# Weighted output rows summed as 512-column identity products, with the top's part added on VectorE

## What is computed

```python
logits = x @ W_in.T + b_in                      # 4 trees, 1365 nodes each, 4 outputs ("fan") a node
act4 = gelu(logits).reshape(B, 4, 1365, 4)
decisions = argmax(act4, axis=-1)               # the child to go to
# walk down 5 levels: 6 visited nodes per tree and row
masked = act4 * visited[..., None]
g = masked.reshape(B, -1) @ W_out.T             # sum of gelu(logit) * output row, over visited nodes
x = x + s * silu(g)
```

## Time and profile before

| | us |
|---|---|
| median of three executions | 2034.4 |
| the profiled execution | 2048.09 |
| its span, first to last instruction | 2046.3 |
| mean granted TensorE clock | 0.890 |
| busy in the span: PE / DVE / POOL / ACT | 1549.5 / 1517.5 / 1301.7 / 1129.3 |

### The profile page before, as it was taken

The page is one execution under the profiler, slowest core; times in us unless marked ns, Lnnn a source line. Parts: engine busy times, 40 slices in busy tenths (PEclk is TensorE's granted clock), DMA queues, the critical chain, the costliest instruction groups (busy, mean ns, idle before and its releaser), DMA issues. The chain is left out here.

```text
span 2046.3 us, 31347 instructions
## 1 busy us (share of the span) xinstructions
PE 1549.5 (76%) x10312; PEld 1086.4 (53%) x10376; DVE 1517.5 (74%) x2701; ACT 1129.3 (55%) x3167; POOL 1301.7 (64%) x1780
## 2 busy tenths in 40 slices
PE   6989898888998748731578777777778777777765
PEld 4667677677776643311355555555555555555543
DVE  2466759677686863995688888888888888888843
ACT  2356566665666733331356666666666666666643
POOL 0455446365555710554888888888888888888700
PEclk9889889998999878965689999999999999999877
DMA  2555565564756814763000000000000000000004
GB/s 84 180 179 205 172 216 193 180 207 166 244 170 207 281 50 128 234 178 112 1 15 3 17 17 17 17 6 12 17 17 17 16 6 12 17 17 17 4 3 123
DMA packets 137573, 191.97 MB, mean 94 GB/s; under 512 B 65730, under 2 KB 94788, under 8 KB 137284
## 3 DMA queue, kind: packets, MB, share of 16 engines
q0 software_dynamic: 36864, 134.76, 19.5%
q1 hardware_dynamic: 95314, 50.98, 9.1%
q10 hardware_dynamic: 5234, 4.23, 0.7%
HBM read 166.22 MB, written 23.72 MB: 93 GB/s over the span
## 5 line engine op out<-in xcount | busy, mean ns | idle before, releaser
L304 POOL DMA_INDIRECT l_rows<-in_table,l_idx x256 | 333.9, 1304 | 294.5 <-DVE l_idx L635 179.4
L437 PE MATMUL l_acc<-l_rows,ident 128*128 128x128 f32 x2048 | 310.4, 307 | 73.9 <-ACT l_rows L531 67.5
L437 PEld LDWEIGHTS l_acc<-l_rows,ident 128*128 128x128 f32 x2048 | 275.8, 214 | 109.1 <-ACT l_rows L531 100.7
L531 ACT ACTIVATE l_rows<-l_rows,l_act 128x128 f32<-128x128 f32 x1024 | 306.1, 387 | 2.1
L1315 ACT ACTIVATE lo_prob<-lo_s_ps,lo_nmx,lo_rn 128x128 f32<-128x128 f32 x512 | 226.7, 460 | 43.5 <-DVE lo_nmx L1579 41.7
L1467 POOL TENSOR_TENSOR lo_c<-lo_c 128x1024 f32<-128x1024 f32 x64 | 150.8, 2356 | 11.2 <-DVE lo_c L1569 6.8
L585 DVE TENSOR_TENSOR l_rows<-l_rows,xn_tok 128x2048 f32<-128x2048 f32 x64 | 145.9, 2279 | 8.5 <-DMA l_rows<-in_table,l_idx 8.5
L586 DVE TENSOR_REDUCE l_dot<-l_rows 128x16 f32<-128x2048 f32 x64 | 146.3, 2286 | 2.2
L403 PE MATMUL l_S<-top_out,l_AT 128*128 128x144 f32 (+3 forms) x832 | 126.4, 301 | 21.6 <-ACT l_AT L522 17.2
L522 ACT ACTIVATE l_AT<-l_log,top_bias 128x512 f32<-128x512 f32 (+1 forms) x96 | 63.9, 684 | 133.4 <-PE l_log L395 118.6
L403 PEld LDWEIGHTS l_S<-top_out,l_AT 128*128 128x128 f32 (+2 forms) x832 | 112.2, 202 | 34.5 <-ACT l_AT L522 22.6
(11 more groups left out here) (266 smaller groups left out, 3972.4 us busy)
## 6 DMA issues: line engine op xcount, KB each, us to landing
scratch_ops<-pr_ops SPq DMA_DIRECT2D x4, 1568.0 KB, 5.7
lo_de_ops<-scratch_ops SPq DMA_DIRECT2D x16, 392.0 KB, 3.7
l_rows<-in_table,l_idx POOLq DMA_INDIRECT x256
lo_de_qo<-scratch_qo SPq DMA_DIRECT2D x16, 256.0 KB, 3.9
x_tok<-in_x SPq DMA_DIRECT2D x8, 256.0 KB, 5.2
scratch_q<-pr_stage_q SPq DMA_DIRECT2D x8, 256.0 KB, 3.8
scratch_k<-pr_stage_k SPq DMA_DIRECT2D x8, 256.0 KB, 2.3
pr_Yq<-scratch_q SPq DMA_DIRECT2D x8, 256.0 KB, 3.0
```

The source lines that it names most:

```text
L304: pool.indirect_dma_start(rows[L][:, r % SLOTS, p, :], None, a[f"table{L}"], bass.IndirectOffsetOnAxis(ap=at[:, p:p + 1], axis=0)).then_in ...
L437: ins = pe.matmul(out, m["ident"][:], rows[L][:, r % SLOTS, p, (FAN + f) * D:(FAN + f + 1) * D], start=False, stop=(L == 5 and k == PICK - ...
L531: ins = act.activation(z, z, ACT.Copy, scale=actv[L][:, r % 2, k:k + 1])
```

## The change

1. A product now spans 512 columns: for each of the 4 trees one product of the identity with the 4 scaled output rows of that tree (4 x 128 columns next to each other). Per tile and level there are 4 products instead of 16. `acc[k]` becomes a bank per tile (alternating by r mod 2), and holds four partial sums of 128 columns each; levels 4 and 5 of a tile add into the same bank.
2. The product of the identity with `ftop` is gone. A new DVE step `total(r)` reduces the four partial sums (128x512 from PSUM, read with a step of 128) to 128 columns in SBUF, and adds them to `ftop` of that tile, in place. It runs in round r+2, after `dots(5, r+1)` and ahead of `scan` and `norms`.
3. `ftop` has 3 group buffers instead of 2. `tanh_f` waits for `total` and reads `ftop` (SBUF); so does the merge.
4. Since levels 4 and 5 of one tile share a bank that only alternates by tile, PE's `spread_rows(4, .)` moves one round later: round r now does `spread_rows(4, r-1)`, in the same place of the round, and `spread_rows(5, r-1)` at its end. It waits for `total(r-3)`.
5. To make room, `t1` and `t2` become halves of `fsum`, and `th` shares the buffer of `n_`.

The gathers' own code is unchanged: `gather(4, r+2)` still waits for `spread_rows(4, r-1)`, with 3 buffers.

```diff
-        acc = [ps(f"l0_acc{k}", [P, GT, D]) for k in (0, 1)]
+        acc = [ps(f"l0_acc{k}", [P, FAN * D]) for k in (0, 1)]
@@ TensorE
             def spread_rows(L, r):
-                h, j = r // GT, r % GT
-                out = acc[h % 2][:, j, :]
-                if L == 4:
-                    if j == 0 and h >= 2:
-                        pe.wait_ge(acc_read.sem, acc_read.after(h - 2))
-                    pe.wait_ge(ftop_kept.sem, ftop_kept.after(h))
-                    pe.matmul(out, m["ident"][:], ftop[:, h % 2, j, :], start=(j == 0), stop=False, skip_group_check=True)
-                for k in range(PICK):
-                    if k % 4 == 0:
-                        pe.wait_ge(scaled[L].sem, scaled[L].after(r, k // 4 + 1))
-                    p, f = k // FAN, k % FAN
-                    ins = pe.matmul(out, m["ident"][:], rows[L][:, r % SLOTS, p, (FAN + f) * D:(FAN + f + 1) * D],
-                                    start=False, stop=(L == 5 and k == PICK - 1), skip_group_check=True)
+                if L == 4 and r >= 2:
+                    pe.wait_ge(acc_read.sem, acc_read.after(r - 2))
+                for p in range(TREES):
+                    pe.wait_ge(scaled[L].sem, scaled[L].after(r, p + 1))
+                    ins = pe.matmul(acc[r % 2][:], m["ident"][:], rows[L][:, r % SLOTS, p, FAN * D:2 * FAN * D],
+                                    start=(L == 4 and p == 0), stop=(L == 5 and p == TREES - 1), skip_group_check=True)
                 ins.then_inc(spread[L].sem, 1)
@@
-                if tile_ok(r):
-                    spread_rows(4, r)
+                if tile_ok(r - 1):
+                    spread_rows(4, r - 1)
@@ ScalarE
             def keep_ftop(h):
-                if h >= 2:
-                    act.wait_ge(spread[4].sem, spread[4].after((h - 1) * GT - 1))
+                if h >= 3:
+                    act.wait_ge(merged.sem, merged.after(h - 3))
@@
             def tanh_f(h):
-                act.wait_ge(spread[5].sem, spread[5].after(h * GT + GT - 1))
+                act.wait_ge(totalled.sem, totalled.after(h * GT + GT - 1))
-                act.activation(t_[:], acc[h % 2][:], ACT.Tanh, scale=0.5).then_inc(t_ready.sem, 1)
+                act.activation(t_[:], ftop[:, h % 3], ACT.Tanh, scale=0.5).then_inc(t_ready.sem, 1)
@@ VectorE
+            def total(r):
+                h, j = r // GT, r % GT
+                dve.wait_ge(spread[5].sem, spread[5].after(r))
+                dve.tensor_reduce(fsum[:, 0:D], acc[r % 2][:].rearrange("p (f d) -> p d f", d=D), AX.X, ALU.add).then_inc(acc_read.sem, 1)
+                dve.wait_ge(acc_read.sem, acc_read.after(r))
+                dve.wait_ge(ftop_kept.sem, ftop_kept.after(h))
+                dve.tensor_tensor(ftop[:, h % 3, j, :], ftop[:, h % 3, j, :], fsum[:, 0:D], ALU.add).then_inc(totalled.sem, 1)
+                dve.wait_ge(totalled.sem, totalled.after(r))
@@
-                    dve.scalar_tensor_tensor(t_[:], t_[:], 1.0, acc[hm % 2][:], ALU.add, ALU.mult).then_inc(acc_read.sem, 1)
-                    dve.wait_ge(acc_read.sem, acc_read.after(hm))
+                    ch.link(dve.scalar_tensor_tensor(t_[:], t_[:], 1.0, ftop[:, hm % 3], ALU.add, ALU.mult))
@@
                 if tile_ok(r - 1):
                     dots(5, r - 1)
+                if tile_ok(r - 2):
+                    total(r - 2)
```

More of the change, by code:

```diff
@@ L198, in layer0_phase @@
         mx, mw = sb("l0_mx", [P, GT * TREES]), sb("l0_mw", [P, GT * TREES])
-        t1, t2 = sb("l0_t1", [P, GT * PICK]), sb("l0_t2", [P, GT * PICK])
+        fsum = sb("l0_fsum", [P, 2 * GT * PICK])
+        t1, t2 = fsum[:, 0:GT * PICK], fsum[:, GT * PICK:]
         rel5 = sb("l0_rel5", [P, TREES])
@@ L205, in layer0_phase @@
         actv = {L: sb(f"l0_act{L}", [P, 2, PICK]) for L in (4, 5)}
-        ftop = sb("l0_ftop", [P, 2, GT, D])
+        ftop = sb("l0_ftop", [P, 3, GT, D])
         halfb = sb("l0_halfb", [P, 4])
@@ L209, in layer0_phase @@
         go = sb("l0_go", [P, 3, GW])
-        n_, th, t_ = (sb("l0_" + k, [P, GT, D]) for k in ("n", "th", "t"))
+        n_, t_ = (sb("l0_" + k, [P, GT, D]) for k in ("n", "t"))
+        th = n_
         w["pen"] = th[:, 0, :]
@@ L240, in layer0_phase @@
         affine, th_ready, t_ready = st("affine"), st("th_ready"), st("t_ready")
-        acc_read, merged, xn1_ready = st("acc_read"), st("merged"), st("xn1_ready")
+        acc_read, totalled, merged, xn1_ready = st("acc_read"), st("totalled"), st("merged"), st("xn1_ready")
         m_turned, m_kept = st("m_turned"), st("m_kept")
@@ L493, in keep_ftop @@
                 act.wait_ge(weighed.sem, POS[h, 11] + 1)
-                if h >= 2:
-                    act.wait_ge(spread[4].sem, spread[4].after((h - 1) * GT - 1))
+                if h >= 3:
+                    act.wait_ge(merged.sem, merged.after(h - 3))
                 act.wait_ge(chosen[3].sem, chosen[3].after(h))
-                act.copy(ftop[:, h % 2, :, :], S[:, :, PICK:PICK + D]).then_inc(ftop_kept.sem, 1)
+                act.copy(ftop[:, h % 3, :, :], S[:, :, PICK:PICK + D]).then_inc(ftop_kept.sem, 1)
             def squash(h, n):
```

## The result

The changed kernel is slower: median 2057.61 us of five executions (2052.75 to 2060.52) against 2034.40 of the kernel before, measured with it (five executions, 2030.2 to 2039.8), ratio 1.0100, 95% interval 1.0074 to 1.0125. Forecast was 2035 with a range to 2049.

The account below looks back on a forecast made before the run. Bound by a chain through several engines, none full. Ramp -6.5, groups -9.6, fifth group +0.9, tail +12.0, half clock +3.4 sum to +0.2 us; carried to the median 2034.6, said as 2035, range 2022 to 2049.

Parts of the forecast that it names:

- The products' price: On PE, per tile and level: four 32-bit products of 512 columns take 3.4 us.
- the gain from the width: On PE: four products of 512 columns instead of sixteen of 128 save 0.34 us per tile and level.
- The price of `total`: On DVE, per tile: reduce 0.69 and add 0.28, each plus 0.04 to the next start, 1.05 us.
- rival 3: On DVE: the strided reduce goes at half rate, +0.7 us per `total` on the chain; +9, 2044; chance 0.10.
- One group: ... choose5(14) 2.6 us early: In each regular group: shorter waits and products bring `choose5(14)` 2.6 us early; gathers limit the gain to 2.4, four groups -9.6.
- rival 2: Half clock falls on level 4's products after PE idles, in tail and groups (r mod 4 = 1): +14, 2048; chance 0.20.
- The gather path: From level 4's products' end through eight POOL gathers to `dots(5, r)`: 0.1 + 12.5 + 4.5 = 17.1 us; just closes in round 13.
- The fifth group: 569 to 647 us: no top left in its last rounds, rows land at 648.1 for `dots(5, 25)`: +0.9 us.
- rival 4: Another wait, such as `scan` behind `sigmoids`, free by 1 us only, takes back 1 to 2 us per group: +6, 2041; chance 0.08.
- Rival 1: Gathers on POOL not stretched by DVE's `dots`, 14.5 us instead of 17.1: -11 us, 2023; chance 0.22.
- The tail: 647 to 775 us: +10.0 for late gathers, +2.0 for `total`, +3.4 for tile 26's products at half clock.
- The ramp: 82 to 219 us: waits removed in the first rounds, part taken back in round 3 by `sigmoids` and `total`: -6.5 us.

Follow-up runs that it names:

- experiment 2: Changed kernel with 16 products of 128 columns instead of 4 of 512 per tile and level: 2053.38 us, ratio 1.0075.
- experiment 1: Kernel before with only level 4's products moved one round later, 128 columns, no `total`: 2044.76 us, ratio 1.0029.
- experiments 10: Kernel before with level 4's products a round later, 4 and 2 gather buffers (levels 4, 5), zero products in rounds r mod 4 = 3: 2016.47 us, ratio 0.9869.
- experiment 6: Changed kernel with 4 and 2 gather buffers for levels 4 and 5, plus zero products in rounds r mod 4 = 3: 2026.87 us, ratio 0.9942.
- experiment 9: Kernel before with level 4's products one round later and 4 and 2 gather buffers, no `total`, 128 columns: 2020.12 us, ratio 0.9878.
- experiment 3: Changed kernel with 4 buffers of gathered rows for level 4 and 2 for level 5, instead of 3 each: 2033.65 us, ratio 0.9975.
- experiment 4: Changed kernel with 4 zero products of 512 columns in PE's gaps, rounds r mod 4 = 3 with top logits: 2047.54 us, ratio 1.0042.
- second trace: Kernel before, run and traced once more with no edit: 2038.66 us, span 2036.9.

## Why the prediction was wrong

The sum missed by 23 us: 12.1 in the four groups, whose sign was wrong, 5.5 in the fifth, 3.0 in the tail, and 6.0 in the ramp, where the traces don't agree with each other, less 3.4 ahead of `dots(4, 0)`. Point by point:

- **The products' price was right, the gain from the width was not.** Four of 512 columns take 3.43 us from their start to the next instruction's, forecast 3.4. But the 3.74 us that I compared it with for sixteen of 128 is a duration to a modelled end; from start to start they take 3.57. The width saves 0.14 us a tile and level, not 0.34, and experiment 2 shows nothing of it. The rows, first of the kernel before, then of the changed one:

```profile
351.36 3.74 PE L437 MATMUL l_acc<-l_rows,ident 128*128 128x128 f32 x32
354.93 0.61 PE L395 MATMUL l_log<-l_pen,l_mask 128*128 128x128 bf16 x8
...
342.03 3.60 PE L432 MATMUL l_acc<-l_rows,ident 128*128 128x512 f32 x8
345.46 0.61 PE L397 MATMUL l_log<-l_pen,l_mask 128*128 128x128 bf16 x8
```

- **The price of `total` was right**, 1.04 us on DVE (299.89 to 300.93; reduce 0.68, add 0.29), and the reading with a step of 128 costs nothing extra: rival 3 falls. What of it lands on the path, 8.6 us (experiment 2 against 1), fits the one per group and the few of ramp and tail that the sum held; with the gathers in time it was 14 to 16 us (experiments 10 against 6, 9 against 3), which the sum doesn't explain.
- **The step that failed: "One group: ... choose5(14) 2.6 us early", -9.6 in the sum.** I let the products run unpaced, took off the waits that they had caused, and kept every other duration. The waits went as said (ACT's gelu of the top begins at 324.93 and 366.29 without one). But unpaced products leave PE idle where they used to stretch over ACT's scaling, and there the clock falls to half: a third low stretch per group, in the middle of the ping-pong of the top, 2.29 for 1.25 us and 1.92 for 1.02. Four groups: +2.5 instead of -9.6. Experiment 4 shows it: with the gaps filled and nothing else changed they take 344.3 us, 7.5 below the kernel before, and 10.1 below with the gathers in time as well (experiment 6). ACT's waits for PE's `penalty`, forecast down by a third, fell only from 120.4 us (second trace) to 100.8. I had a rival for the clock (the second), and at 0.20 and at the wrong place: I put it on level 4's products in rounds r mod 4 = 1, and it came in r mod 4 = 3 behind them.
- **The gather path was right in mechanism and too short by 1 to 2 us, so that it "just closes" only on paper.** From the first of the eight gathers to the dots that wait for the last I had 12.5 + 4.5 = 17.0 us; it was 18.6 in round 13 (rows below) and 17.9 and 18.8 in the tail (685.27 to 703.16, 703.22 to 722.05). The eight took 12.9, 13.3 and 13.8, the landing 5.7, 4.6 and 5.0.

```profile
366.15 0.93 POOL L306 DMA_INDIRECT l_rows<-in_table,l_idx  x1 [8.78 <-PE l_acc L432]
...
384.74 2.29 DVE L580 TENSOR_TENSOR l_rows<-l_rows,xn_tok 128x2048 f32<-128x2048 f32 x1 [0.98 <-DMA l_rows<-in_table,l_idx]
```

  In round 13 `dots(5, 13)` waited 0.98 us for data (forecast 0.2), in round 11 `scan` waited 1.15 us for `sigmoids` (forecast free by 1 us). The fifth group cost +6.4 instead of +0.9, and experiment 3 gives 5.5 of it back, so it is the gathers. The wait for `sigmoids` is that of rival 4; the half clock on level 4's products in the groups, rival 2, isn't what came. Rival 1 falls: gathers are stretched by L580 (2.46, 3.03 and 3.04 us in the tail).
- **The tail came near for partly wrong reasons**: +15.4, measured +18.4. I had 10.0 for the gathers, 3.4 for the clock and 2.0 for `total`. The gathers are 11.3 (experiment 3), and 7.1 stay with the buffers; without `total` and the wide products nothing stays (experiment 9, 126.5). So `total` was the term too small: eight of them run in the tail, between the dots on which the next indices and gathers hang, and I had counted two. The clock was too large: the products of tile 26 took 5.20 us (at 663.18) instead of 3.60, 1.6 and not 3.4. The two misses in part cancel.
- **The ramp** was to gain 6.5 us and gained 0.5 by the table, but this miss isn't shown. Three traces of the old order have 136.8, 130.3 and 136.7 us, on average 134.6; the changed kernel's 129.8 is 0.5 below the lowest and 4.8 below the average. The ten traces of kernels with the change or a part of it run from 122.6 to 133.3. Single traces can't settle a gain of this size.
- **Against the rule on the gathers** ("SBUF — State Buffer", "Who interferes with whom", in the Trainium skill: by that section a tensor_tensor did not stall descriptor generation, for a reason that it marks as inferred; it also says that a VectorE instruction with two SBUF inputs contends with a GpSimd instruction that reads SBUF) the trace of the changed kernel repeats and sides with the second sentence: the gather at 703.22 begins 0.06 us behind an L580 at 703.16 and lasts 3.04 us, until 0.81 us after its end. All 35 gathers of this trace that begin while an L580 runs end 0.80 to 0.86 us after it (58 in the kernel before, 0.80 to 0.87).

What stays open: whether the width itself costs up to 5 us, why the price of `total` grows when the gathers are in time, and what the ramp gains.

## What to carry to other kernels

Taking a wait off TensorE is not the same as taking time off: if what is left is a gap, look at what runs behind the gap and price it at the half clock, and if that loses, fill the gap with products that change nothing. When a step that frees a buffer is moved a round later, count the buffers in the same breath: here one more for level 4, taken from level 5, turned +6 us into -21. And when a path closes to within 1 us on paper, sum it as if it didn't.

## What the runs showed of the hardware

- Two idle gaps of PE of 1.30 and 2.64 us, with 0.62 us of mask products between them, were followed by a fall of the granted clock from 1.00 to 0.63 and 0.52 in the windows behind; with the gaps filled by products of the identity with zeros it stayed at 1.00 (experiment 4). Gaps of 0.93 and 2.64 us behind products of 128 columns had the same effect (experiment 1). The Trainium skill, "TensorE: Matmul & The Clock Gate", section "Why this matters for your kernels", advises against gaps of PE of more than about 3 us between bursts. Here each gap is shorter than that, and the two lie close to each other.
- A 32-bit product of 512 columns costs PE 0.86 us and four of 128 columns 0.89 us, both from start to start at the full clock (3.43 us for four, 3.57 for sixteen), so width buys 4%.
- A reduce of 128x512 from PSUM that reads with a step of 128 took DVE 0.68 us, and a step over 128x512 read in order 0.69.
- Eight indirect gathers in a row took 9.7 us where next to none was held up (from 299.13 in the changed kernel) and 12.5 to 13.8 where two were; their data came 4.5 to 5.7 us after the last. One that begins while VectorE runs the 128x2048 tensor_tensor of two SBUF inputs ends 0.80 to 0.87 us after it (93 of 93 in the first trace of the kernel before and that of the changed one). One that has begun ahead of it mostly isn't held up: all 18 of the changed kernel that began up to 0.75 us ahead took 0.93 to 1.02 us; in the kernel before 29 of 31 took 0.93 to 1.05, and two that began 0.11 us ahead took 3.25.
